# Second attention layer: keys of ten sequences projected around the expert stage and kept on chip

## Chip, cores and metric

One core of one Trainium2 chip. The metric is the device time of one execution in microseconds. Three executions of the kernel before took 968.67, 968.87 and 966.95 us, median 968.67 us. The engines are named as the profile names them: PE (TensorE matmul), PEld (its weight load), DVE (VectorE), ACT (ScalarE), POOL (GpSimd), SP (SyncE, here the main issuer of transfers).

## What is computed

The input is 32 sequences of 128 tokens of width 128 (`x`) and a context of the same shape. Two layers follow each other, each a cross attention and a feed-forward part, each with a layer norm ahead of it and a residual sum behind it. Layer 0: 16 heads of 8 columns, then top-2 of 8 experts (128 to 512 to 128). Layer 1, the one that the change is about:

```python
kv = context @ Wkv
k, v = jnp.split(kv, 2, axis=-1)
q = x @ Wq                                  # 16 heads of 64 columns: 1024 wide
dots = jnp.einsum('bhnd,bhmd->bhnm', q, k) * SCALE
dots = dots - (1.0 - mask.astype(jnp.float32))[:, None, :, None] * MASK_NEG
attn = jax.nn.softmax(dots, axis=-1)
out = jnp.einsum('bhnm,bhmd->bhnd', attn, v)
return out.transpose(0, 2, 1, 3).reshape(b, n, h * d) @ Wout + bout
```

and a feed-forward part of width 512. The keys of layer 1 depend on the context and on `Wkv` alone, not on `x`.

## The kernel before, in words

Everything is fp32. Each engine has its own program, written out by hand; semaphores (`x_ge` waits with counts) tie them together, and each engine works strictly in the order written. There are four stages.

1. **First layer** (`step0`, 32 sequences, a pipeline of some seven steps). Each step also projects the second layer's values of one sequence and stores them in DRAM (`v_dram`). SP loads weights for later stages between blocks of steps (`late_loads`).
2. **First passage.** DVE counts rows for each expert and works out the first tile of each (`tile_start`, L896 to L915), ACT and SP zero the last tile of each expert's rows in DRAM (`zero_last_tile`, L317: a register load and a 128 KB transfer each), PE turns the query mask (L1200), waits for `rt["tiles"]` and loads nine tile counts into registers (L1211), transposes the first tile (`transpose_tile`, L1206) and starts.
3. **Experts** (L1213 to L1227): 35 tiles of 256 rows. PE works as a chain of L1219 (first product), L1206 (transpose of the next tile) and L1226 (second product); ACT applies relu (L685).
4. **Second passage** and **second layer** (`step1`). POOL gathers expert outputs (L563), DVE adds them to `X` (L954) and normalizes; then the steps run.

In `step1`, step n of PE runs, in this order: first half of the scores of sequence n (L1254, S_BANK), a transpose of probabilities (`transpose_unit`, L1066), the output product of n-2 (L1281), the second feed-forward product of n-3 (L1291), another L1066, the transposes of the normalized rows and of the context of n+1 (`transpose_in`, L1056 and L1058), second half of the scores, L1066, the projections `project_y` of n+1 (L1242), the transpose of n-2 for the feed-forward part (L1339), first half of attention times values of n-1 (`values`, L1264), L1066 of n, the second half of L1264, and the first feed-forward product (L1363). `project_y(q, g)` is four matmuls of 128x128 by 128x128; g = 0 and 1 give the keys, g = 2 and 3 the queries. DVE reads each g out of PSUM with `read_y` (L949) into `YT`: g = 0, 1 and then, in the next step, g = 2, 3. g uses banks 4, 5, 6, 4; the two halves of `values` use banks 5 and 6, so they wait until DVE has read g = 1 and g = 2.

ACT's order in a step: copy of transposed probabilities, `fill_rows` (L616, the mask and the move of scores from PSUM to `PR`), `exponentials` (L609) of units 2 and 3 of the sequence before, `read_heads` (L694), `fill_rows` of units 0 and 1, `read_xct` (L597, transposed rows and context), `exponentials` of units 0 and 1 of this one, `fill_rows` of unit 2. DVE takes row maxima (`row_max`, L786), `sums_reciprocal` (L791); POOL scales the probabilities (`scale_pool`, L327). `over_steps` writes the first and last steps out and loops over pairs in between: in `step1` steps -3 to 5 are written out, 6 to 27 are the loop.

## Time and profile before

| | |
|---|---|
| median of three executions | 968.67 us |
| the profiled execution's own time | 973.7 us |
| its span, first to last instruction | 972.1 us |
| PE busy | 903.8 us, 93% of the span |
| DVE, ACT, POOL busy | 675.3, 674.9, 442.4 us |
| mean granted PE clock | 0.977 of full speed |
| first layer, to PE's last piece of it | 0 to 344.3 us |
| first passage (PE without work) | 344.6 to 355.7 us |
| experts | 355.7 to 491.7 us |
| second passage (PE without work) | 491.7 to 502.8 us |
| second layer | 502.8 to 972.1 us |

A row of a timeline gives the start in us, the busy time in us, engine, line of the kernel, operation, output and input tiles with shapes and how many instructions were merged; in brackets stands how long the engine sat idle before it and what released it. An fp32 matmul of 128x128 by 128x128 stands as two records (L1242: 16 matmuls for each of 32 sequences, 1024 records), a transpose as one. Ends of matmuls are modelled: the distance of starts tells more than the duration.

### The profile page before, as it was taken

Reading aid. Unit: us, or ns where it says so; the run is one execution under the profiler, and the core shown is the slowest. Engines: PE = TensorE matmul, PEld = TensorE weight load, DVE = VectorE, ACT = ScalarE, POOL = GpSimd, SP = SyncE. Lnnn points to the kernel's source line nnn. Section 1 sums busy time; section 2 is a strip of 40 time slices with the busy share of each in tenths; the row PEclk is TensorE's granted clock in tenths of the full one; section 3 lists DMA queues with packets and bytes.
Section 4 is the critical chain, followed back from the end, with each engine's and each line's share of the span. In section 5 each row is a group of like instructions: output and inputs, shape, how many; then the busy total and the mean of one; then the engine's idle time right before and its main releaser. Section 6 shows DMA issues by size and latency. Waiting matters only on the chain. (4 is left out here: it accounts for less than half of the span.)

```text
span 972.1 us, 30288 instructions
## 1 busy us (share of the span) xinstructions
PE 903.8 (93%) x8399; PEld 786.3 (81%) x8399; DVE 675.3 (69%) x2169; ACT 674.9 (69%) x2666; POOL 442.4 (46%) x732
## 2 busy tenths in 40 slices
PE   3899999999999849999948999999999999999996
PEld 2577777777777639999947899999999999999986
DVE  5689989899987742222237777777777777777763
ACT  1799989989998703332308877877787787778782
POOL 4033444444343421111145666666666656666542
PEclk9999999999999959999979999999999999999998
DMA  4766667666766222222221121212111211211110
GB/s 136 213 214 209 218 195 233 208 217 208 238 204 208 71 77 72 70 71 70 65 70 58 48 62 59 63 43 65 54 53 54 62 57 43 65 57 62 36 51 9
DMA packets 115276, 103.74 MB, mean 107 GB/s; under 512 B 11921, under 2 KB 102579, under 8 KB 115222
## 3 DMA queue, kind: packets, MB, share of 16 engines
q1 hardware_dynamic: 106754, 88.81, 29.4%
q0 software_dynamic: 5776, 12.99, 4.4%
q10 hardware_dynamic: 2692, 1.31, 0.5%
q8 instruction: 24, 0.39, 0.2%
q14 instruction: 30, 0.25, 0.1%
HBM read 56.53 MB, written 46.53 MB: 106 GB/s over the span
## 5 line engine op out<-in xcount | busy, mean ns | idle before, releaser
L609 ACT ACTIVATE PR<-PR,nmx 128x128 f32<-128x128 f32 x512 | 197.7, 391 | 2.6 <-DVE nmx L786 2.6
L327 POOL TENSOR_TENSOR PR<-PR,rden 128x512 f32<-128x512 f32 x128 | 133.9, 1046 | 129.0 <-DVE rden L791 129.0
L609 ACT ACTIVATE PR<-bank,nmx 128x128 f32<-128x128 f32 x512 | 182.5, 385 | 7.4 <-issue 5.6
L1066 PE MATMUL bank<-ident,PR 128*128 128x128 f32 x1024 | 161.0, 281 | 2.5 <-DVE w L797 1.2
L1066 PEld LDWEIGHTS bank<-ident,PR 128*128 128x128 f32 x1024 | 114.5, 141 | 57.7 <-issue 42.2
L949 DVE COPY YT<-bank 128x512 f32<-128x512 f32 x128 | 84.3, 678 | 56.5 <-PE bank L1242 56.2
L1242 PE MATMUL bank<-XCT,wqk 128*128 128x128 f32 x1024 | 121.4, 277 | 0.5 <-ACT XCT L597 0.5
L1242 PEld LDWEIGHTS bank<-XCT,wqk 128*128 128x128 f32 x1024 | 118.5, 194 | 1.0 <-ACT XCT L597 0.9
L609 ACT ACTIVATION_READ_ACCUMULATOR PR<-bank,nmx 128x1 f32 x512 | 114.5, 224 | 0.0
L685 ACT ACTIVATE H<-bank 128x512 f32<-128x512 f32 x70 | 41.8, 597 | 102.7 <-PE bank L1219 102.7
L786 DVE TENSOR_REDUCE nmx<-bank 128x4 f32<-128x512 f32 x128 | 86.6, 677 | 18.4 <-PE bank L1084 17.8
L609 ACT ACTIVATION_READ_ACCUMULATOR PR<-PR,nmx 128x1 f32 x512 | 98.1, 192 | 0.0
L786 DVE TENSOR_REDUCE nmx<-PR 128x4 f32<-128x512 f32 x128 | 86.4, 676 | 11.0 <-ACT PR L616 11.0
L616 ACT ACTIVATE PR<-bank,fill_q 128x512 f32<-128x512 f32 x128 | 83.9, 679 | 11.1 <-PE bank L1254 7.6
L563 POOL DMA_INDIRECT QF<-expert_outputs,gidx x64 | 65.4, 1022 | 36.5 <-POOL gidx L560 24.4
L597 ACT ACTIVATE XCT<-bank 128x256 f32<-128x256 f32 x64 | 24.6, 385 | 81.8 <-PE bank L1058 81.3
L290 POOL TENSOR_TENSOR rstd<-veps,expo 128x1 f32<-128x1 f32 x128 | 73.2, 572 | 14.6 <-POOL veps L287 8.0
L287 POOL TENSOR_SCALAR veps<-mv 128x1 f32<-128x1 f32 x128 | 29.4, 229 | 104.0 <-DVE mv L303 95.0
L1254 PE MATMUL bank<-YT 64*128 64x128 f32 x1024 | 74.4, 285 | 2.4 <-DVE YT L949 1.2
L1084 PE MATMUL bank<-KBD,QS 128*128 128x512 f32 x128 | 76.2, 595 | 0.0
L549 POOL DMA_DIRECT2D expert_outputs<-PR x35 | 19.0, 543 | 124.6 <-DVE PR L940 124.6
L539 POOL DMA_INDIRECT expert_inputs<-wide,scat_idx x64 | 66.0, 1031 | 16.7 <-issue 10.0
(177 smaller groups left out, 2068.8 us busy)
## 6 DMA issues: line engine op xcount, KB each, us to landing
second_layer_values<-wide SPq DMA_DIRECT2D x32, 512.0 KB, 3.2
wide<-second_layer_values SPq DMA_DIRECT2D x32, 512.0 KB, 3.2
expert_outputs<-HF SPq DMA_DIRECT2D x32, 256.0 KB
expert_outputs<-HF SPq DMA_DIRECT2D x64, 128.0 KB, 1.9
KBD<-expert_outputs SPq DMA_DIRECT2D x128, 64.0 KB
QS<-expert_outputs SPq DMA_DIRECT2D x32, 256.0 KB
PR<-expert_inputs SPq DMA_DIRECT2D x36, 128.0 KB, 2.0
expert_outputs<-PR POOLq DMA_DIRECT2D x35, 128.0 KB, 2.0
```

The lines of the kernel that those rows point to most:

```text
L290: nc.gpsimd.tensor_tensor(rstd[:, p, :], veps[:, p, :], expo[:], ALU.pow).then_inc(s["rstd"], 1)
L327: nc.gpsimd.tensor_tensor(unit, unit, rden[:, p, G * g:G * g + G].unsqueeze(2).broadcast_to([P, G, P]), ALU.mult).then_inc(s["nm"], 1)
L539: nc.gpsimd.indirect_dma_start(xs, bass.IndirectOffsetOnAxis(scat_idx[:, p, k:k + 1], 0), XK[:, p, :], None).then_inc(rt[f"sc{p}"], 16)
L563: nc.gpsimd.indirect_dma_start(GY[:, q, i, :], None, ys, bass.IndirectOffsetOnAxis(gidx[:, q, i:i + 1], 0)).then_inc(mix[f"g{q}"], 16)
L609: last = nc.scalar.activation(PR[:, g, j * P:(j + 1) * P], scored, ACT.Exp, bias=nmx[:, p, h:h + 1], accum_out=den[:, p, h:h + 1])
L616: nc.scalar.activation(PR[:, g, :], S_BANK[g % 2][:], ACT.Identity, bias=fill_q[:, bass.ds(m, 1)]).then_inc(c["sh"], 1)
L786: nc.vector.tensor_reduce(nmx[:, p, G * g:G * g + G], scored.rearrange("p (j k) -> p j k", j=G), AXX, ALU.max, negate=True).then_inc(s["mx ...
L949: nc.vector.tensor_copy(YT[:, p, G * g:G * g + G, :].rearrange("p h s -> p (h s)"), Y_BANK[g][:]).then_inc(c["yc"], 1)
L1066: last = nc.tensor.transpose(T_BANK[g % 2][:, j * P:(j + 1) * P], PR[:, g, j * P:(j + 1) * P], ident[:])
L1084: mm(S_BANK[g % 2][:], QS[:, p, g, :], KBD[:, p, g, :, :].rearrange("p j s -> p (j s)"), start=False, stop=True, skip_group_check=True).th ...
L1242: last = mm(Y_BANK[g][:, j * P:(j + 1) * P], wqk1[:, 1 - g // 2, chunk * P:(chunk + 1) * P], XCT[:, p, 1 - g // 2, :], start=True, stop=True)
L1254: last = mm(S_BANK[r][:, j * P:(j + 1) * P], QT1[half, p, chunk, :], KT1[half, p, chunk, :], start=True, stop=True)
```

## The change

For sequences 0 to 9 (`early`) the keys of layer 1 are no longer projected in their step but ahead of the second layer, by a new function `keys_ahead`, and stay on chip: those of 0 to 4 in the first passage (`KEYS`, in the place of two first-layer tiles), those of 5 to 9 in the second (in the expert weights' tiles `w2` and `w1`). Each group transposes five contexts, ACT copies them to `CT`, 40 matmuls project the keys, and ACT moves each half of a sequence's keys out of PSUM (`read_keys`). Two transfers of 320 KB bring the contexts, into the tiles of the key masks that are no longer read. In their steps these ten sequences transpose no context, project g = 2 and 3 only, and DVE reads only these; everything else keeps its order. ACT does the keys of sequences 1 to 4 between the zeroing transfers. Ten steps of `step1` instead of six (steps -3 to 9) are written out, the loop starts at 10. Some semaphores are merged, with no other effect. Shown with what is left out marked by "...":

```diff
+KEYS_A = 5
+KEYS_AHEAD = 10
...
+        with ExitStack() as first_layer:
+            KBD = first_layer.enter_context(nc.sbuf_tensor("KBD", [P, 2, NU, G, P], FP32R))
+            QS = first_layer.enter_context(nc.sbuf_tensor("QS", [P, 2, NU, P], FP32R))
+        KEYS = sb("KEYS", [P, KEYS_A, PAIRS, P])
...
+        CTX_A, CTX_B = (t[:].bitcast(FP32).rearrange("p (k d) -> p k d", d=P) for t in (mk3, mk_bc))
+        CT = H[:].rearrange("p a c s -> p (a c) s")
+
+        def early(m):
+
+            return isinstance(m, int) and m < KEYS_AHEAD
+
+        def key_slot(m):
+
+            if m < KEYS_A:
+                return KEYS[:, m, :, :]
+            if m < 9:
+                return w2[:, 2 * (m - 5):2 * (m - 5) + 2, :, :].rearrange("p e c d -> p (e c) d")
+            return w1[:, 4:6, :].rearrange("p e (c d) -> p (e c) d", d=P)
...
+                    sp.wait_ge(set_copy, 3)
+                    sp.dma_start(CTX_A[:, 0:KEYS_A, :], ctx_in[0:KEYS_A].rearrange("b s d -> s b d")).then_inc(ld_kv, 16)
...
+            sp.wait_ge(a["kc"], NB)
+            sp.dma_start(CTX_B[:, 0:KEYS_AHEAD - KEYS_A, :],
+                         ctx_in[KEYS_A:KEYS_AHEAD].rearrange("b s d -> s b d")).then_inc(ld_gate, 16)
             sp.wait_ge(rows_zeroed, 3)
             sp.wait_ge(rt["counts"], 1)
...
-                if exists(n + 2):
+                if exists(n + 2) and not early(n + 2):
...
+            act.wait_ge(wo_strips, 2)
+            nc.scalar.activation(fill_q[:], bank[0][:, 0:NB], ACT.Copy).then_inc(parts_ready, 1)
+            def read_keys(m, half):
+
+                act.wait_ge(kg["k"], 2 * m + half + 1)
+                out = (bank[6], bank[5])[half] if m < KEYS_A else bank[half]
+                nc.scalar.activation(key_slot(m)[:, 4 * half:4 * half + 4, :].rearrange("p c s -> p (c s)"), out[:],
+                                     ACT.Copy).then_inc(kg["kc"], 1)
+
+            def read_contexts(group, fifth):
+
+                act.wait_ge(set_pe, group + 3)
+                nc.scalar.activation(CT[:, 0:4, :].rearrange("p c s -> p (c s)"), bank[3][:], ACT.Copy)
+                nc.scalar.activation(CT[:, 4, :], fifth[:, 0:P], ACT.Copy).then_inc(set_copy, 1)
+
+            read_contexts(0, bank[4])
+            read_keys(0, 0)
+            read_keys(0, 1)
+            act.wait_ge(rt["counts"], 2)
             nc.scalar.activation(egap[:], gap[:], ACT.Exp).then_inc(rt["egap"], 1)
-
-
             act.wait_ge(rows_zeroed, 3)
             act.wait_ge(rt["counts"], 1)
             for e in range(1, NE):
                 zero_last_tile(act, e)
+                if e < KEYS_A:
+                    read_keys(e, 0)
+                    read_keys(e, 1)
...
+            read_contexts(1, bank[6])
+            for m in range(KEYS_A, KEYS_AHEAD):
+                for half in range(2):
+                    read_keys(m, half)
...
-                    read_xct(c, n + 1, q, True, c["y"], NU * (n))
+                    read_xct(c, n + 1, q, not early(n + 1), c["y"], NU * (n))
...
-                if exists(n + 1):
+                if exists(n + 1) and not early(n + 1):
                     read_y(n + 1, q, 0)
...
+            def keys_ahead(group, first, last, contexts, fifth, out):
+
+                pe.wait_ge(ld_kv if group == 0 else ld_gate, 32)
+                for i in range(last - first):
+                    turned = nc.tensor.transpose((bank[3][:, i * P:(i + 1) * P] if i < 4 else fifth[:, 0:P]), contexts[:, i, :], ident[:])
+                turned.then_inc(set_pe, 1)
+                pe.wait_ge(set_copy, group + 4)
+                for m in range(first, last):
+                    for half in range(2):
+                        if m > first:
+                            pe.wait_ge(kg["kc"], 2 * m + half - 1)
+                        for j in range(G):
+                            chunk = G * half + j
+                            projected = mm(out[half][:, j * P:(j + 1) * P], wqk1[:, 1, chunk * P:(chunk + 1) * P],
+                                           CT[:, m - first, :], start=True, stop=True)
+                        projected.then_inc(kg["k"], 1)
+
+            pe.wait_ge(ld_w1, 12 * 16)
+            pe.wait_ge(a["x"], NB)
+            pe.wait_ge(a["pjv"], 2 * NB)
+            keys_ahead(0, 0, KEYS_A, CTX_A, bank[4], (bank[6], bank[5]))
...
             transpose_tile(0)
+            pe.wait_ge(kg["kc"], 2 * KEYS_A)
...
+            keys_ahead(1, KEYS_A, KEYS_AHEAD, CTX_B, bank[6], (bank[0], bank[1]))
...
+                    keys = key_slot(m) if early(m) else KT1[:, p, :, :]
+                    if isinstance(m, int) and m == 0:
+                        pe.wait_ge(kg["kc"], 2 * KEYS_AHEAD)
...
-                    transpose_in(c, n + 1, q, True)
+                    transpose_in(c, n + 1, q, not early(n + 1))
...
+                if exists(n + 1) and not early(n + 1):
...
+                    project_y(n + 1, q, 0)
...
+                    project_y(n + 1, q, 1)
                 if exists(n + 1):
...
+                    project_y(n + 1, q, 2)
...
+                    project_y(n + 1, q, 3)
...
-            over_steps(pe, step1, -3, NB + 2, 3, 6)
+            over_steps(pe, step1, -3, NB + 2, 3, KEYS_AHEAD)
```

## Rows read from the trace of the kernel before

**Rows 1.** The page, busy time of the engines, and PE in 40 slices.

```profile
PE 903.8 (93%) x8399; PEld 786.3 (81%) x8399; DVE 675.3 (69%) x2169; ACT 674.9 (69%) x2666; POOL 442.4 (46%) x732
...
PE   3899999999999849999948999999999999999996
```

**Rows 2.** Steps 0 to 4 and 7 of the second layer: window, length, busy time, clock.

```profile
510.24:518.72 8.48, 6.90 (x70) 6.21 (x70) 6.01 (x15) 7.05 (x28) 3.09 (x6) 1.00 0.24 77
518.72:530.30 11.58, 10.42 (x115) 9.17 (x115) 9.86 (x24) 10.70 (x42) 8.05 (x12) 1.00 0.07 18
530.30:544.20 13.90, 13.44 (x141) 12.05 (x139) 10.97 (x25) 11.92 (x45) 8.98 (x13) 1.00 0.18 55
...
558.30:572.94 14.64, 14.17 (x148) 12.97 (x147) 10.65 (x29) 11.14 (x43) 8.19 (x12) 1.00 0.17 55
...
601.14:615.24 14.10, 14.10 (x148) 12.89 (x147) 10.62 (x31) 10.98 (x43) 8.80 (x13) 1.00 0.19 58
```

**Rows 3.** Timeline of PE in step 7 of the second layer.

```profile
605.84 0.27 PE L1056 MATMUL bank<-ident,XN 128*128 128x128 f32 x1
605.95 0.27 PE L1058 MATMUL bank<-ident,CX 128*128 128x128 f32 x1
...
607.74 3.74 PE L1242 MATMUL bank<-XCT,wqk 128*128 128x128 f32 x32
...
611.52 1.09 PE L1264 MATMUL bank<-w,wide 128*64 128x128 f32 x16
...
613.13 1.09 PE L1264 MATMUL bank<-w,wide 128*64 128x128 f32 x16
```

**Rows 4.** Timelines of ACT and DVE in step 7.

```profile
606.26 0.39 ACT L597 ACTIVATE XCT<-bank 128x256 f32<-128x256 f32 x1 [2.04 <-PE bank L1058]
...
609.62 0.67 ACT L616 ACTIVATE PR<-bank,fill_q 128x512 f32<-128x512 f32 x1
...
611.04 1.25 DVE L949 COPY YT<-bank 128x512 f32<-128x512 f32 x2
```

**Rows 5.** First passage: timelines of PE, then of ACT.

```profile
344.32 0.31 PE L1200 MATMUL bank<-ident,mq_f 32*128 32x32 f32 x1
355.73 0.68 PE L1206 MATMUL bank<-ident,PR 128*128 128x128 f32 x2 [11.10 <-issue]
356.93 3.79 PE L1219 MATMUL bank<-PR,w 128*128 128x128 f32 x16 [0.51 <-DVE PR L932]
...
346.57 7.52 ACTq L320 DMA_DIRECT2D expert_inputs<-zero  x7
```

**Rows 6.** Register loads of PE's nine tile counts and of ACT's zeroing; columns: duration ns, first and last start.

```profile
L1211 PEldq TENSOR_LOAD <-tile_start x9: 299/317/502, 349.3 to 355.1; - x9
...
L319 ACTq TENSOR_LOAD <-fill_row x7: 279/300/485, 345.7 to 352.8; - x7
```

**Rows 7.** Second passage and head of the second layer: timeline of PE.

```profile
489.73 1.95 PE L1226 MATMUL bank<-w,H 128*128 128x128 f32 x16
502.84 0.45 PE L1056 MATMUL bank<-ident,XN 128*128 128x128 f32 x1 [11.16 <-DVE XN L295]
...
503.98 5.48 PE L1242 MATMUL bank<-XCT,wqk 128*128 128x128 f32 x32 [0.47 <-ACT XCT L597]
510.24 1.16 PE L1254 MATMUL bank<-YT 64*128 64x128 f32 x16 [0.78 <-DVE YT L949]
```

**Rows 8.** Head of the second layer: timelines of POOL and DVE.

```profile
506.43 0.57 POOL L290 TENSOR_TENSOR rstd<-veps,expo 128x1 f32<-128x1 f32 x1
...
510.10 0.34 DVE L295 TENSOR_SCALAR XN<-X,mv,rstd 128x128 f32<-128x128 f32 x1
...
512.21 1.28 DVE L786 TENSOR_REDUCE nmx<-PR 128x4 f32<-128x512 f32 x2 [0.35 <-ACT PR L616]
```

**Rows 9.** Windows with the granted clock (third column from the right), both passages.

```profile
360.00:361.00 1.00, 1.00 (x8) 1.00 (x7) 0.00 (x0) 0.25 (x1) 0.00 (x0) 0.66 0.00 0
...
492.00:496.00 4.00, 0.00 (x0) 0.00 (x0) 0.01 (x1) 0.00 (x0) 0.82 (x3) 0.72 0.09 33
```

More of the change, by code:

```diff
@@ L668, in _ @@
             nc.scalar.activation(wqk1[:, 0, :], wqk1[:, 0, :], ACT.Copy, scale=float(DH1) ** -0.5).then_inc(wq_scaled, 1)
-            act.wait_ge(c_turned, 1)
-            nc.scalar.activation(fill_q[:], bank[0][:, 0:NB], ACT.Copy).then_inc(c_stored, 1)
-            act.wait_ge(rt["gap"], 1)
+            act.wait_ge(wo_strips, 2)
[13 more added lines that the diff above has]
+            act.wait_ge(rt["counts"], 2)
             nc.scalar.activation(egap[:], gap[:], ACT.Exp).then_inc(rt["egap"], 1)
@@ L897, in _ @@
             nc.vector.tensor_copy(fill_row[:], next_row[:]).then_inc(rt["counts"], 1)
-            nc.vector.tensor_tensor(gap[:], topv[:, 1, :], topv[:, 0, :], ALU.subtract).then_inc(rt["gap"], 1)
+            nc.vector.tensor_tensor(gap[:], topv[:, 1, :], topv[:, 0, :], ALU.subtract).then_inc(rt["counts"], 1)
             link(nc.vector.tensor_tensor(place[:], next_row[:], region[:], ALU.subtract))
@@ L949, in read_y @@
                     nc.vector.tensor_copy(YT[:, p, G * g:G * g + G, :].rearrange("p h s -> p (h s)"),
-                                          Y_BANK[g][:]).then_inc(c["yc"], 1)
+                                          Y_BANK[g][:]).then_inc(c["yc"], 3 if g == 2 and early(m) else 1)
                 def add_experts(m, p, i, done):
@@ L1243, in project_y @@
                                   XCT[:, p, 1 - g // 2, :], start=True, stop=True)
-                    last.then_inc(c["y"], 1)
+                    last.then_inc(c["y"], 3 if g == 2 and early(m) else 1)
                 def scores(m, p, pair):
+                    keys = key_slot(m) if early(m) else KT1[:, p, :, :]
+                    if isinstance(m, int) and m == 0:
+                        pe.wait_ge(kg["kc"], 2 * KEYS_AHEAD)
                     wait(pe, c["yc"], NU * m + NU)
@@ L1253, in scores @@
                             half = slice(DH1 * r, DH1 * r + DH1)
-                            last = mm(S_BANK[r][:, j * P:(j + 1) * P], QT1[half, p, chunk, :], KT1[half, p, chunk, :],
+                            last = mm(S_BANK[r][:, j * P:(j + 1) * P], QT1[half, p, chunk, :], keys[half, chunk, :],
                                       start=True, stop=True)
@@ L1287, in step1 @@
                         wait(pe, c["yc"], upto(n, 4, 3))
-                        wait(pe, c["yc"], upto(n, 4, 0))
+                        if not early(n):
+                            wait(pe, c["yc"], upto(n, 4, 0))
                         wait(pe, d["x"], upto(n - 4))
@@ L1307, in step1 @@
                     transpose_unit(c, n - 1, 3)
-                if exists(n + 1):
+                if exists(n + 1) and not early(n + 1):
                     pe.wait_ge(c["xct"], n + 2)
@@ L1313, in step1 @@
                         wait(pe, c["yc"], upto(n, 4, 3))
-                        wait(pe, c["yc"], upto(n, 4, 0))
-                    project_y(q, 0)
+                        if not early(n):
+                            wait(pe, c["yc"], upto(n, 4, 0))
+                    project_y(n + 1, q, 0)
                     pe.wait_ge(c["xct"], n + 2)
@@ L1318, in step1 @@
                     if isinstance(n, int):
-                        wait(pe, c["yc"], upto(n, 4, 1))
-                    project_y(q, 1)
+                        if not early(n):
+                            wait(pe, c["yc"], upto(n, 4, 1))
+                    project_y(n + 1, q, 1)
+                if exists(n + 1):
                     pe.wait_ge(c["xct"], n + 2)
@@ L1324, in step1 @@
                         wait(pe, c["yc"], upto(n, 4, 2))
-                    project_y(q, 2)
+                    project_y(n + 1, q, 2)
                     pe.wait_ge(c["xct"], n + 2)
-                    wait(pe, c["yc"], upto(n + 1, 4, 0))
+                    if not early(n + 1):
+                        wait(pe, c["yc"], upto(n + 1, 4, 0))
                     if isinstance(n, int):
@@ L1343, in step1 @@
                     pe.wait_ge(c[f"v{q}"], loads(n - 1, q))
-                    wait(pe, c["yc"], upto(n + 1, 4, 1))
+                    if not early(n + 1):
+                        wait(pe, c["yc"], upto(n + 1, 4, 1))
                     if isinstance(n, int):
@@ L1358, in step1 @@
                     if isinstance(n, int):
-                        wait(pe, c["yc"], upto(n + 1, 4, 0))
+                        if not early(n + 1):
+                            wait(pe, c["yc"], upto(n + 1, 4, 0))
                         wait(pe, d["x"], upto(n - 3))
```

39 lines of the change are left out of this document (18 added, 21 removed).

## The prediction

> **What bounds the kernel now.** I read first the page's busy times and slices: PE is busy 93% of the span and falls off in two places only, the passages before and after the experts [rows 1]. Then the windows over single steps of the second layer: from step 3 on PE is busy for all of a step's 14.10 us, while ACT has 10.98, DVE 10.62 and POOL 8.80 us of work [rows 2]. So a step costs what PE issues in it. Steps 0 to 2 differ: 8.48, 11.58 and 13.90 us, PE busy for 6.90, 10.42 and 13.44; in step 1 it is ACT (10.70 of 11.58) that hardly rests [rows 2]. Third, the timelines of the passages: PE does nothing for 11.1 us in each [rows 5, 7]. The first gap is not all free time. Its releaser reads "issue", and the rows of PE's sequencer say why: the nine tile counts are loaded one after another, from 349.3 to 355.1 us, 5.8 us for eight intervals or 0.72 us for each, 6.5 in all, and the first tile is transposed 0.2 us behind the last [rows 5, 6]. The second gap waits for POOL and DVE, up to the first normalized rows at 502.84 [rows 7].
>
> **A step of an early sequence.** Removed from PE: two of four projections, 16 of 32 records. 32 of them take 3.58 us by their starts (3.74 with the modelled end), 0.112 us each, so 1.79 us; and the context's transpose, 0.11 us (605.84 to 605.95) [rows 3]. Together 1.90 us. From DVE go two reads of 0.6 us, from SP a transfer, from ACT half of a small copy; none bounds a full step. Does the whole 1.90 arrive? The second half of L1264 writes the bank from which DVE must have read the first query half. DVE reads that behind a row maximum which needs ACT's `fill_rows`; ACT starts that at 609.62 behind eight exponentials, which start behind the copy at 606.26, which hangs on PE's transpose at 605.84 [rows 3, 4]. That chain keeps its length, but for 0.1 us of a shorter copy: the pair of reads starts at 611.04, the first is done at about 611.67, in the new step at 611.55. PE would be at this L1264 at 613.13 - 1.90 = 611.23 [rows 3]. It waits 0.3 us and a semaphore's passage, say 0.4. So a full early step becomes 12.6 us, a gain of 1.5; ACT with 10.9 of 12.6 still fits. Bounds: 1.9 without that wait, and 0.4 if the others of the queue (transposes behind POOL's scaling, L1254 behind the reads) come short too.
>
> **The sum over the second layer.** The projections of sequence 0 stand in step -1, those of 1 to 9 in steps 0 to 8. *Head:* the first queries are projected warm, 16 x 0.112 = 1.8 us instead of 5.48 [rows 7], so the first scores could start some 4.2 us earlier. But the row maxima behind them stand in DVE's order behind the normalization of sequence 1, which POOL's root allows at 506.43 + 0.57 = 507.0; it happened at 510.10, and the maxima at 512.21 [rows 8]. 2.11 us separate these two, 0.35 of it idle, so the maxima come at about 507.05 + 1.8 = 508.85, 3.4 us earlier. From there ACT works without rest, and step 1 starts 3.4 us earlier. *Step 1* is ACT's: 11.58 goes to 10.3, near its own work; 1.2. *Step 2:* PE's 13.44 less 1.90 is 11.54, and 0.2 of waits: 2.2. *Steps 3 to 8:* six times 1.5, and the 0.5 us that step 4 has over the others (14.64), which comes from a late read that more slack lets vanish: 9.5 [rows 2]. Sum 16.3 us gained. Bounds: 19 with no wait in full steps, 12 with 0.8 a step.
>
> **First passage.** All of `keys_ahead(0)` stands in PE's order ahead of the nine register loads, and these no longer run beside DVE's and POOL's work. From 344.63 [rows 5]: five transposes, at the lower level of the clock (1.2 of 2.4 GHz), for PE was nearly idle before. The first tile, behind its gap, shows what that costs: its first 16 records took 3.58 us (356.93 to the successor's start at 360.51), 0.22 each, and the clock rose in the window 360 to 361 (0.66), 3.5 us into dense products [rows 5, 9]. So 1.1 us; then ACT's two copies, 0.9 us with passages: 346.6. Of 80 records 16 run slow (3.5 us, to 350.1) and 64 at 0.112 (7.2 us): 357.3. ACT reads the keys between zeroings, one in 7.1/6 = 1.18 us, most of it register load, which I let its sequencer run ahead of the copies [rows 5, 6]; for a sequence that is 1.2 beside two copies of some 0.5, against PE's 1.8. I add 0.5: 357.8. Then 6.5 us of loads, 364.3, and the first tile's transposes at 364.4 instead of 355.73: 8.7 us lost. ACT's last three zeroings end at about 361.5, under cover of the loads. The clock will have dropped again, as it began to after the last expert product (0.72 in 492 to 496) [rows 9], so the first tile is slow as before: no change. Bounds: 4.5, if the loads begin under PE's products, and 11 if each zeroing stands in series with its copies (2.2 us a sequence).
>
> The profile shows the loads only with PE idle [rows 6], so I have them begin when the products end. The Trainium skill, in "TensorE: Matmul & The Clock Gate" ("Architectural detail: the array is 16x 32x32"), says that TensorE's queue is 64 deep, so that its sequencer may run on while products are queued. By that the loads would overlap the last half's eight records, and the passage would cost 0.9 us less; no row here shows it.
>
> **Second passage.** PE ends the experts at 491.6. Five transposes 0.6, ACT's copies and passages 0.9: 493.1. 80 records at 0.112 are 9.0 us: 502.1, against 502.75, when the first rows are ready [rows 7]. It fits, with 0.65 us to spare, if the clock stays up over a rest of 1 us; with it up, the head above runs fast. ACT's ten copies of 0.6 us hide beside PE's 0.9 each, the last done at 502.8, before `read_xct` needs ACT. Cost nothing; if one of these is longer by 1 us, up to 0.5. The transfers: 320 KB in the first layer and 320 KB at its end, where SP is idle; two issues, no waiter: nothing, bound 1 us.
>
> **Sum.** -16.3 + 8.7 = -7.6 us. The profiled execution took 973.7 us itself (972.1 of span), 5.0 over the median; it would be 966.1, and the median 968.67 - 7.6 = **961.1 us**.
>
> **Rivals.**
> *A: the loads or the slow clock cost less than I think.* If PE's sequencer passes the products, or the clock is up from the start, the first passage costs 4.5 us. For it: ACT's loads for the zeroings stand in its sequencer's rows, not in its engine's [rows 6]. Against: PE's waits for `kc` hold its sequencer to the last half. With the full 1.9 a step in half of the steps: -4.5 - 14 = -13.5 and so 956.5 or less. 0.2.
> *B: the clock stays low.* If waits for ACT keep it at 1.2 GHz over both groups, the first ends at 345 + 19 + 6.5 = 370.5, 14.8 us late, and in the second 80 records take 17.9, 8.3 us past the rows. -16.3 + 14.8 + 8.3 = +6.8: 975.5. Against: in both PE is dense for its first 3.5 us, and comes into the second at full clock. 0.03. Only the first of them low: -16.3 + 14.8 = -1.5, 967.2; 0.05.
> *C, the slow side: the freed time in the steps turns into the wait at L1264.* The place is the second half of `values`, behind the chain transpose, copy, eight exponentials, `fill_rows`, maximum, read. Its price: if a full step gives 0.2 and steps 1 and 2 give 0.5 together, the layer gives 3.4 + 0.5 + 1.2 = 5.1, and 8.7 - 5.1 = +3.6: 972.3. It decides against the change from where steps 1 to 8 together gain under 5.3 us, 0.66 a step. For it: ACT's slack falls from 3.1 to 1.7 us a step. Against: the chain, timed row by row, leaves only 0.4. 0.1.
> *D: the gain and the price cancel*, 4 us less in steps and 3 more in the passage: about 968. 0.1.
>
> **How the numbers follow.** Forecast 0.52, A 0.2, C 0.1, D 0.1, B 0.03 and its milder form 0.05. The range for 8 in 10: the forecast with its bounds (12 to 19 gained, 7 to 11 lost: 956.7 to 967.7), and most of A: 955.5 to 967.7. 0.2% is 1.9 us, about what a measurement can tell from no change. Faster by over that (below 966.7): forecast and A, and a little of D, 0.74; within it: the rest of D and B's milder form, 0.13; slower (over 970.6): C and B, 0.13.
>
> **What would show it.** In the changed profile: L1211's loads start at 357 to 358 and the first L1206 comes at 364 to 365; the second keys' products end at 502 to 503 on a scale moved by this, and L1056 follows 11 us behind the last L1226; the first maximum is 9 us behind the first L1056 before and 6 after; steps 3 to 8 last 12.6 us with a wait for YT before the second L1264; from step 9 14.10 again. I am wrong if the first tile comes within 3 us of 355.7, if early steps last over 13.4, or if the second passage grows.

## The result: 0.5% slower, and the profile after

The changed kernel takes 973.85 us (median of 7 executions, 971.04 to 974.91) against 968.67 us (966.95 to 969.53): ratio 1.0052, 95% interval 1.0038 to 1.0067, that is 3.7 to 6.5 us more. The forecast was 961.1 us, 7.6 less. The profiled execution took 973.05 us itself, span 971.3 us. It seems shorter than the one shown of before (973.7), but that one was 5 us over its own median, in its first layer: that layer ended at 344.3 us, and in the trace of **e7** below, which shares it, at 340.3. So the two traces are compared piece by piece.

| piece, by the starts of PE's instructions | before, us | after, us | difference | forecast |
|---|---|---|---|---|
| the query mask's turn to the first tile's transpose | 11.41 | 19.74 | +8.3 | +8.7 |
| experts | 134.00 | 133.76 | -0.2 | 0 |
| last second product to the first normalized rows | 13.11 | 14.98 | +1.9 | 0 |
| head and step 0 of the second layer | 15.88 | 12.80 | -3.1 | -3.4 |
| step 1 | 11.58 | 10.88 | -0.7 | -1.2 |
| step 2 | 13.90 | 13.62 | -0.3 | -2.2 |
| steps 3 to 8 | 85.14 | 81.39 | -3.8 | -9.5 |
| from step 9 | 342.7 | 342.7 | 0.0 | 0 |

They sum to +2.1 us. In the first layer a single step is longer, 11.3 us instead of 9.4: together +4.0 us, inside the measured interval. The page after, busy times and PE in 40 slices:

```profile
PE 908.8 (94%) x8399; PEld 790.6 (81%) x8399; DVE 667.3 (69%) x2149; ACT 686.5 (71%) x2690; POOL 441.6 (45%) x732
...
PE   3899999999999769999988889999999999999997
```

PE is busier than before [rows 1], for the same 8399 instructions; work was moved, none left out. The lines of the kernel have moved too. L1256 and L1265 are the transposes and the products of `keys_ahead`, L1284 the register loads (L1211 before), L1279, L1293 and L1300 the experts' (L1206, L1219, L1226), and in the second layer L1107, L1318, L1333, L1343 and L1423 are what L1056, L1242, L1254, L1264 and L1339 were. In the experiments all of them shift by a few lines more. The first passage on PE's timeline, and then the register loads (duration in ns, first and last start):

```profile
341.43 0.31 PE L1251 MATMUL bank<-ident,mq_f 32*128 32x32 f32 x1
341.67 1.33 PE L1256 MATMUL bank<-ident,mk 128*128 128x128 f32 x5
343.85 11.84 PE L1265 MATMUL bank<-H,wqk 128*128 128x128 f32 x80 [0.85 <-ACT H L709]
361.17 0.69 PE L1279 MATMUL bank<-ident,PR 128*128 128x128 f32 x2 [5.48 <-issue]
```

```profile
L1284 PEldq TENSOR_LOAD <-tile_start x9: 293/306/539, 354.7 to 360.5; - x9
```

As forecast, the keys fill the gap of [rows 5] and the nine loads of [rows 6] stand behind them, 5.8 us from the first to the last as before, now with DVE and POOL at rest and ACT done at 359.2. They begin at 354.7 while the 80 records run to 355.7: PE's sequencer runs 1.0 us ahead of its products. The Trainium skill gives TensorE a queue 64 deep ("TensorE: Matmul & The Clock Gate", "Architectural detail: the array is 16x 32x32"), which would have made the passage 0.9 us cheaper than my sum. The overlap agrees with that; how deep the queue is, no run here shows.

Second passage and head: PE, then DVE and SP.

```profile
496.71 0.71 PE L1256 MATMUL bank<-ident,mk_bc 128*128 128x128 f32 x5
498.28 9.44 PE L1265 MATMUL bank<-H,wqk 128*128 128x128 f32 x80 [0.85 <-ACT H L709]
509.91 0.30 PE L1107 MATMUL bank<-ident,XN 128*128 128x128 f32 x1 [2.20 <-DVE XN L302]
510.58 2.05 PE L1318 MATMUL bank<-XCT,wqk 128*128 128x128 f32 x16 [0.37 <-ACT XCT L624]
513.51 1.16 PE L1333 MATMUL bank<-KEYS,YT 64*128 64x128 f32 x16 [0.88 <-DVE YT L1000]
```

```profile
498.55 0.49 DVE L991 COPY PR<-bank 128x128 f32<-128x128 f32 x2 [2.92 <-DMA expert_outputs<-PR]
```

```profile
493.40 0.81 SPq L505 DMA_DIRECT2D wide<-second_layer_values  x2
```

The keys cost nothing here: PE is done 2.2 us before the rows come. But the rows come 1.9 us later than in [rows 7], because DVE waits 2.9 us for a store of expert outputs before it can empty the last tile. At that time two loads of values, 512 KB each, are under way. Before, the first of them was issued at 503.9, 14.2 us behind the last second product; now both are issued ahead of it. The landing times, after and then before (last column, median us):

```profile
wide<-second_layer_values SPq DMA_DIRECT2D x2, 512.0 KB, 4.0
expert_outputs<-PR POOLq DMA_DIRECT2D x2, 128.0 KB, 3.2
```

```profile
expert_outputs<-PR POOLq DMA_DIRECT2D x2, 128.0 KB, 2.0
CX<-in_ctx_dram SPq DMA_DIRECT2D x2, 64.0 KB, 1.9
```

Windows over steps 0, 1, 2, 4, 7 and 10 of the second layer, after (window, length, busy PE, PEld, DVE, ACT, POOL, clock, DMA), and PE in step 7:

```profile
513.51:522.71 9.20, 7.99 (x54) 7.15 (x54) 4.87 (x13) 7.41 (x29) 6.05 (x9) 0.63 0.06 18
522.71:533.59 10.88, 8.59 (x99) 7.29 (x98) 8.23 (x19) 10.16 (x40) 7.39 (x10) 1.00 0.04 12
533.59:547.21 13.62, 11.70 (x125) 10.21 (x123) 10.30 (x26) 11.81 (x45) 9.45 (x14) 1.00 0.16 51
560.49:575.36 14.87, 12.42 (x132) 11.07 (x131) 10.18 (x28) 11.03 (x43) 8.79 (x14) 1.00 0.16 52
601.98:615.29 13.31, 12.42 (x131) 11.07 (x130) 10.20 (x28) 10.94 (x43) 8.80 (x14) 1.00 0.20 61
642.70:656.80 14.10, 14.10 (x149) 12.89 (x149) 10.63 (x31) 10.98 (x43) 8.80 (x13) 1.00 0.19 58
```

```profile
608.47 1.95 PE L1318 MATMUL bank<-XCT,wqk 128*128 128x128 f32 x16
611.31 0.33 PE L1423 MATMUL bank<-ident,XND 128*128 128x128 f32 x1 [0.89 <-DVE XND L317]
611.57 1.09 PE L1343 MATMUL bank<-w,wide 128*64 128x128 f32 x16
```

Against [rows 2] step 7 lost 0.79 us of length where PE lost 1.68 of busy time. PE waits 0.89 us, and it waits at L1423, ahead of the first L1343, not at the second as forecast. L1423 transposes `XND`, the normalized rows of sequence n-2 that go into its feed-forward part. What the wait is for is to be read from POOL, DVE and ACT in the same step:

```profile
606.45 1.08 POOL L590 DMA_INDIRECT QF<-expert_outputs,gidx  x1 [0.79 <-POOL gidx L587]
607.84 0.96 POOL L590 DMA_INDIRECT QF<-expert_outputs,gidx  x1 [0.30 <-issue]
...
609.57 0.57 POOL L297 TENSOR_TENSOR rstd<-veps,expo 128x1 f32<-128x1 f32 x1
610.14 1.03 POOL L334 TENSOR_TENSOR PR<-PR,rden 128x512 f32<-128x512 f32 x1
```

```profile
610.18 1.07 DVE L317 TENSOR_SCALAR XND<-X,mv,rstd 128x128 f32<-128x128 f32 x1 [1.17 <-POOL rstd L297]
```

```profile
610.24 0.67 ACT L643 ACTIVATE PR<-bank,fill_q 128x512 f32<-128x512 f32 x1
610.81 0.58 ACT L650 ACTIVATE w<-bank 128x512 f32<-128x512 f32 x1
```

Two things hold PE up, and they arrive 0.1 us apart. XND needs POOL's norm, and POOL does it behind two gathers; it is written at 611.25. And the first L1343 needs all transposed probabilities of n-1, whose last copy (L650) stands in ACT's order behind eight exponentials and `fill_rows`; it is done at 611.39. Before, PE came to L1264 at 611.52, 5.7 us behind its L1056 (605.84), with both ready; now it could come 3.9 us behind and comes 4.9 behind (611.57, with L1107 at 606.68). The same two rows before, in step 7:

```profile
609.53 0.32 DVE L310 TENSOR_SCALAR XND<-X,mv,rstd 128x128 f32 x1
610.19 0.58 ACT L623 ACTIVATE w<-bank 128x512 f32<-128x512 f32 x1
```

XND took 0.32 us there and takes 1.07 in every one of the changed kernel's steps 2 to 8, where POOL's scaling (L334) begins 0.05 us ahead of it. So 0.75 of the 0.89 us that PE waits for XND is XND's own length, and ACT's copy would hold PE almost as long. The copy is of the fourth unit, which only the second half of L1343 reads; the program lets the first half wait for all four. No run tried a narrower wait.

### The profile page after: what moved, and what is told of

It reads as the page before. It is cut to its first block and busy times, and to the rows that moved or that the text cites. A ratio compares the mean times of both kernels' runs of the same rounds, so it can differ in the third digit from the quotient of the medians.

```text
span 971.3 us, 30078 instructions
## 1 busy us (share of the span) xinstructions
PE 908.8 (94%) x8399; PEld 790.6 (81%) x8399; DVE 667.3 (69%) x2149; ACT 686.5 (71%) x2690; POOL 441.6 (45%) x732
## 5 line engine op out<-in xcount | busy, mean ns | idle before, releaser
L334 POOL TENSOR_TENSOR PR<-PR,rden 128x512 f32<-128x512 f32 x128 | 133.7, 1044 | 122.1 <-DVE rden L842 122.0
L1318 PE MATMUL bank<-XCT,wqk 128*128 128x128 f32 x864 | 103.7, 278 | 0.4 <-ACT XCT L624 0.4
L1318 PEld LDWEIGHTS bank<-XCT,wqk 128*128 128x128 f32 x864 | 100.6, 195 | 0.8 <-ACT XCT L624 0.6
L837 DVE TENSOR_REDUCE nmx<-bank 128x4 f32<-128x512 f32 x128 | 86.6, 677 | 16.9 <-PE bank L1135 16.2
L1000 DVE COPY YT<-bank 128x512 f32<-128x512 f32 x108 | 70.7, 677 | 39.0 <-PE bank L1318 38.9
L837 DVE TENSOR_REDUCE nmx<-PR 128x4 f32<-128x512 f32 x128 | 86.4, 676 | 12.3 <-ACT PR L643 12.2
L624 ACT ACTIVATE XCT<-bank 128x256 f32<-128x256 f32 (+1 forms) x64 | 23.5, 367 | 69.7 <-PE bank L1109 55.2
L1343 PE MATMUL bank<-w,wide 128*64 128x128 f32 x1024 | 69.8, 279 | 1.1 <-issue 1.1
```

The lines of the kernel that those rows point to most:

```text
L334: nc.gpsimd.tensor_tensor(unit, unit, rden[:, p, G * g:G * g + G].unsqueeze(2).broadcast_to([P, G, P]), ALU.mult).then_inc(s["nm"], 1)
L837: nc.vector.tensor_reduce(nmx[:, p, G * g:G * g + G], scored.rearrange("p (j k) -> p j k", j=G), AXX, ALU.max, negate=True).then_inc(s["mx ...
L1000: nc.vector.tensor_copy(YT[:, p, G * g:G * g + G, :].rearrange("p h s -> p (h s)"), Y_BANK[g][:]).then_inc(c["yc"], 3 if g == 2 and early( ...
L1318: last = mm(Y_BANK[g][:, j * P:(j + 1) * P], wqk1[:, 1 - g // 2, chunk * P:(chunk + 1) * P], XCT[:, p, 1 - g // 2, :], start=True, stop=True)
L1343: last = mm(bank[5 + pair][half, j * P:(j + 1) * P], V1[:, p, 2 * (G * pair + j) + r, :], PTC[:, 2 * pair + r, j * P:(j + 1) * P], start=T ...
```

## The experiments

Ratios are to the kernel before on the same chip, with 95% intervals. Chips differ: before took 968.7 us on the first, 986.5 on that of the second set, 969.5, 970.3 and 985.4 on the next; the difference is in the first layer (on that of the second set it ended at 357.4 instead of 344.3 us), the rest is equal to 0.1 us a step.

### Where the time is: before once more, values held back, counts late

**e0_before_again** is the kernel before, unedited.

> The kernel before, unchanged, profiled and timed once more. The medians say that the change costs 5.2 us, while the two traces, laid over each other by the events of PE, give -2.9 us in the first layer, +8.3 in the first passage, +1.9 in the second, -7.8 in the second layer. Theory: the first trace of before had a first layer 3 to 5 us longer than usual; a new trace of the same kernel then ends its first layer at 339 to 341.5 us instead of 344.3, and the ratio is 1.000 within 0.002. Rival: first layers of before always end at about 344, and the change makes something else slower that the two traces do not show.

Ratio 1.0001 (0.9987 to 1.0015). Passage 11.23, second passage 13.11, steps 14.10: these repeat. The first layer cannot be compared, as the chip was another. What it was meant to test is settled by e7 below, which has the first layer of before on a chip where before takes 969.5 us: it ended at 340.32, not 344.32. The changed kernel's ended at 341.43 in its trace and at 340.8 to 345.9 in those of e5, e8, e9 and e10, so traces of one kernel differ by some 4 us there.

**e1_hold_values**

```diff
                 if exists(n + 2) and not early(n + 2):
                     load_ctx(sp, c, n + 2, p)
+                elif exists(n):
+                    wait(sp, c["tr"], n + 1)
```

> The changed kernel, with SP again holding each of the first loads of values until the transpose that released it before (the context load that carried this wait is gone). Theory: the two loads of 512 KB at 493.4 us stood in the way of the last stores of the expert outputs, which DVE and POOL wait for; held back, the second passage shrinks from 15.0 to 13.1 us and the time falls by 1.9 us against the changed kernel (973.85), to about 972. Rival: the passage grew because ACT or PE is busy with keys; then it stays at 15.0.

Ratio 1.0018 (1.0007 to 1.0030) where the change has 1.0052. The second passage is 13.16 us, and POOL's stores come every 3.79 us up to the last, which in the changed kernel came 5.63 us behind the one before (494.17 to 499.80):

```profile
513.88 0.54 POOL L578 DMA_DIRECT2D expert_outputs<-PR  x1 [3.25 <-DVE PR L993]
517.67 0.54 POOL L578 DMA_DIRECT2D expert_outputs<-PR  x1 [3.25 <-DVE PR L993]
```

The passage's 1.8 us (14.98 to 13.16) are shown to be the two loads. The ratio fell by 3.3 us, more than that; the two intervals leave room for it. The context loads that the change took away had carried the wait that kept the values behind them.

**e3_late_counts**

```diff
-            starts = [pe.value_load(tile_start[0:1, e:e + 1], ...) for e in range(NE + 1)]
+            low = pe.value_load(tile_start[0:1, 0:1], ...)
             transpose_tile(0)
...
             for e in range(NE):
-                with pe.Fori(starts[e], starts[e + 1]) as t:
+                high = pe.value_load(tile_start[0:1, e + 1:e + 2], ...)
+                with pe.Fori(low, high) as t:
...
+                low = high
```

> The changed kernel, with PE loading only the first two tile counts ahead of the experts and each further one ahead of its expert's loop. Theory: the nine loads in series behind the keys are 6.5 us of the first passage's 19.7; with two of them left it is 14.7, and each of the seven moved loads shows for at most 0.7 us between two experts, less what queued products hide: 1 to 5 us less than the changed kernel in all. Rival: the first passage waits for ACT's keys, its zeroing or the transfer of the first tile; then it stays at 18 or more.

Ratio 1.0010 (0.9996 to 1.0025). The first passage is 13.92 us instead of 19.74: the loads were 5.8 us of its growth. The experts take 135.0 us instead of 133.8, but with unedited experts they take 133.6 to 135.0 too, by how long the clock stays at 1.2 GHz in the first tile (5.3 to 6.7 us to the second). What the moved loads give back is read from the tiles behind it: 14 of them last 3.83 to 3.87 us instead of 3.79, 0.9 us in all. That is 4.1 us less than the changed kernel by the ratio, as expected.

### The held steps: four orders of POOL, then ACT and DVE

**e2_pool_order**

```diff
+                if exists(n - 2):
+                    norm_pool(pool, d, n - 2, p)
+                if exists(n) and exists(n - 2):
+                    scale_pool(pool, c, n, p, 0)
                 if exists(n + 3):
                     ...                      # the gathers
...
-                if exists(n - 2):
-                    norm_pool(pool, d, n - 2, p)
-                if exists(n):
+                if exists(n) and not exists(n - 2):
                     scale_pool(pool, c, n, p, 0)
```

> The changed kernel; in each step of the second layer POOL does the norm of n-2 and the first scaling of n ahead of the two gathers, not behind them. Theory: early steps last 13.31 us instead of 12.2 because XND waits for POOL, which stands in two gathers of 3.3 us; with this order the wait of 0.9 us ahead of L1423 vanishes and early full steps last 12.4 to 12.7 us, steps behind them 14.10 as before: 5 to 6 us less than the changed kernel, about 968. Rival: the next wait (ACT's chain to the queries' read, at the second L1343) takes its place at the same length; then steps stay at 13.3.

1027.87 us on a chip where before takes 986.5, ratio 1.042 (1.040 to 1.044). The expectation would be some 986 us there: a miss by 42 us. Early steps last 14.1 to 16.2, late ones 15.1 to 16.2 us. From 600 to 800 us DVE waits for the gathers once, 0.2 us, so they are not what is late. It waits for POOL's second norm, that of a later sequence, for which it doesn't wait there in the changed kernel. The waits of e2 from 700 to 800 us:

```profile
DVE XN L302 <- POOL rstd L297: 14.3, 6, 2.4
```

In this order the scaling stands ahead of the gathers and of that norm, and POOL waits at its scalings for DVE's reciprocals (up to 2.5 us), so all behind it comes late. This is read from the waits; no run tried the norm without the scaling.

**e5_gathers_last** and **e7_before_gathers_last**: the gathers at the end of POOL's step, from step 0 on, in the changed kernel and in that of before.

```diff
-                if exists(n + 3):
+                def gather():
                     ...                      # index copy and both gathers
+                late = not isinstance(n, int) or n >= 0
+                if exists(n + 3) and not late:
                     gather()
...
                     nc.gpsimd.tensor_tensor(xrow, xrow, out_bias[:, 1, :], ALU.add).then_inc(d["bias"], 1)
+                if exists(n + 3) and late:
+                    gather()
```

> The changed kernel; from step 0 on POOL issues its two gathers at the end of a step instead of behind the first scaling. (With the norm and a scaling moved ahead of them, every step of the layer had become longer, 14.2 to 16.2 us.) Theory: XND no longer waits for the gathers, the norm of n-2 is done about 2 us earlier, and the wait ahead of L1423 goes: early full steps last 12.3 to 12.7 us, late steps 14.10; 4 to 6 us less than the changed kernel, ratio to before 1.000 plus or minus 0.001. Rival: XND is late because of the output product and DVE, or the next wait takes its place; then early steps stay at 13.3.

> The kernel before with the same move of POOL's gathers as in e5_gathers_last. Theory: its full steps are PE's, 14.10 us with XND ready 1.5 us ahead of its use, so the order of POOL changes nothing: ratio 1.000 plus or minus 0.001, steps 14.10. Rival: gathers cost steps of the kernel before too, and what e5 gains has nothing to do with the change; then this one gains as much.

Ratios 1.194 (1.192 to 1.197) and 1.191 (1.189 to 1.194): steps of some 20 us in both. The waits of e7 from 600 to 700 us name it:

```profile
DVE X L961 <- DMA QF<-expert_outputs,gidx: 34.0, 5, 7.9
```

```profile
642.39 0.35 DVE L961 SCALAR_TENSOR_TENSOR X<-QF,gate,X 128x128 f32 x1 [6.60 <-DMA QF<-expert_outputs,gidx]
```

DVE adds the gathered rows ahead of much else in its order. It is free for that at 635.8 us, and POOL issues these gathers at 638.25 and 639.63; every step waits up to 7.9 us for them. Both expectations were wrong: the end of POOL's step, taken as early enough, is too late for DVE. No run put the gathers earlier.

**e8_norm_between_gathers** (only in steps with an early next sequence), **e9_copy_early** and **e10_three_orders** (both, and the queries' first half read where the keys' was):

```diff
# e8, POOL
                     for i in range(2):
                         nc.gpsimd.indirect_dma_start(GY[:, q, i, :], ...)
+                        if i == 0 and early(n + 1) and exists(n - 2):
+                            norm_pool(pool, d, n - 2, p)
...
-                if exists(n - 2):
+                if exists(n - 2) and not early(n + 1):
                     norm_pool(pool, d, n - 2, p)
# e9, ACT
-                if exists(n - 2):
+                if exists(n - 2) and not early(n):
                     read_PT(c, n - 2, 3)
...
                     exponentials(c, n, p, 0)
+                if exists(n - 1) and early(n + 1):
+                    read_PT(c, n - 1, 3)
# e10, DVE besides
-                    read_y(n, p, 2)
+                    if not early(n):
+                        read_y(n, p, 2)
...
-                if exists(n + 1) and not early(n + 1):
-                    read_y(n + 1, q, 1)
+                if exists(n + 1):
+                    read_y(n + 1, q, 2 if early(n + 1) else 1)
```

> The changed kernel; in steps whose next sequence is early, POOL does the norm of n-2 between its two gathers (gathers moved to the end of a step came too late for DVE's sum, which waited 8 us for them). Theory of two waits: an early step is held by two things that arrive within 0.1 us of each other, XND (POOL's norm behind both gathers; DVE at 611.25 in the changed trace) and ACT's copy of transposed probabilities (L650, done 611.38), for the first L1343 at 611.57. Freeing XND alone gives nothing: steps 5 to 8 stay within 13.1 to 13.3 us. Rival: XND alone holds the step; then steps are 12.3 to 12.7 us. Step 4's 14.87 stays (a POOL pause of 2.3 us ahead of its gather).

> The changed kernel; in early steps ACT makes the copy of the fourth unit's transposed probabilities between its two groups of exponentials instead of behind fill_rows. Theory of two waits: alone it gives nothing either, since XND is still late: steps 5 to 8 at 13.2 to 13.5 us. Rival: ACT's copy alone holds the step; then steps are 12.8 or less.

> Both moves together, and DVE reads the first query half in the place where it read the first key half. Theory of two waits: now PE finds XND, the copy and the queries' read ready, and an early full step is 12.2 to 12.6 us: 0.7 to 1.1 us a step, 5 to 7 us less than the changed kernel in all, ratio 0.998 to 1.000. Rival: a further chain (ACT's 10.9 us of work a step, or POOL's scaling) holds the step near 13; then the gain is under 2.5 us.

| | step 2 | 3 | 4 | 5 | 6 | 7 | 8 | ratio |
|---|---|---|---|---|---|---|---|---|
| changed | 13.62 | 13.28 | 14.87 | 13.31 | 13.31 | 13.31 | 13.31 | 1.0052 |
| e8 | 12.51 | 13.29 | 13.42 | 13.23 | 13.23 | 13.24 | 13.23 | 1.0018 (1.0003 to 1.0033) |
| e9 | 13.69 | 13.28 | 15.17 | 13.34 | 13.55 | 13.33 | 13.57 | 1.0072 (1.0044 to 1.0100) |
| e10 | 12.44 | 12.32 | 15.93 | 12.20 | 12.95 | 12.34 | 12.80 | 0.9997 (0.9979 to 1.0015) |

Each alone leaves a full step where it was (e9's sixth and eighth are 0.2 us longer), both (with the read) take 0.4 to 1.1 us off steps 3 and 5 to 8; 12.2 to 12.6 was expected, and three of the five are in it. In e10 PE goes through without a stop to the first values:

```profile
610.71 1.95 PE L1324 MATMUL bank<-XCT,wqk 128*128 128x128 f32 x16
612.50 0.27 PE L1429 MATMUL bank<-ident,XND 128*128 128x128 f32 x1
612.70 1.09 PE L1349 MATMUL bank<-w,wide 128*64 128x128 f32 x16
```

In its even steps something third holds PE, a transpose that waits for POOL's scaling. Step 6:

```profile
601.52 0.66 PE L1123 MATMUL bank<-ident,PR 128*128 128x128 f32 x4 [0.64 <-POOL PR L334]
```

Step 4 keeps a pause of POOL (below), and behind PE's waits there the clock is at 1.2 GHz for some 3 us; with the same orders step 4 of e11 stays at full clock and lasts 14.37. Step 4 of e10:

```profile
563.14:579.07 15.93, 14.05 (x131) 12.32 (x130) 12.01 (x31) 12.20 (x47) 10.27 (x15) 0.89 0.19 55
```

The traces show the two waits one by one. In e9 the copy is early, and PE waits for XND as before (step 7). In step 5 of e8 XND is done at 582.52, 1 us before PE asks for it, and PE waits as long for ACT's copy. The steps are 13.33 and 13.23 us:

```profile
614.51 0.33 PE L1426 MATMUL bank<-ident,XND 128*128 128x128 f32 x1 [0.91 <-DVE XND L317]
```

```profile
582.17 0.35 DVE L317 TENSOR_SCALAR XND<-X,mv,rstd 128x128 f32<-128x128 f32 x1
584.06 0.58 ACT L652 ACTIVATE w<-bank 128x512 f32<-128x512 f32 x1
584.74 1.09 PE L1345 MATMUL bank<-w,wide 128*64 128x128 f32 x16 [0.96 <-issue]
```

In steps 3 and 6 to 8 of e8 XND is not free. It starts 1.3 us earlier against the step, but ends only 0.1 earlier. DVE and POOL of step 7:

```profile
608.64 2.25 DVE L317 TENSOR_SCALAR XND<-X,mv,rstd 128x128 f32<-128x128 f32 x1
```

```profile
608.24 1.08 POOL L590 DMA_INDIRECT QF<-expert_outputs,gidx  x1 [0.19 <-issue]
609.34 0.47 POOL L597 TENSOR_TENSOR X<-X,out_bias 128x128 f32<-128x128 f32 x1
609.75 1.05 POOL L334 TENSOR_TENSOR PR<-PR,rden 128x512 f32<-128x512 f32 x1
```

An instruction of 0.3 us lasts 2.25 us and ends with POOL's third in a row; in the changed kernel it lasted 1.07, beside one L334, and in e10 0.34, begun while POOL rested. The Trainium skill, "SBUF — State Buffer" ("Who interferes with whom"), says that DVE in a two-port mode and POOL take one pair of ports for a whole instruction and the other is blocked. The rows agree, and show besides that the blocked one can miss several in a row; in which mode XND runs, they don't show. So freeing XND pays nothing while the copy is late (e8, steps 4 and 5), freeing the copy pays nothing while XND is late (e9), and both pay together (e10). How much of e10 is the DVE read was not tried apart. The 3.3 us by which e8 is faster than the changed kernel come from steps 2 and 4, against its expectation for step 4.

### The parts of the change: first group out, contexts late

**e4_no_first_group**: `KEYS_AHEAD = 5`, `KEYS_A = 0`; no group ahead of the experts, the five sequences behind them.

```diff
-KEYS_A = 5
-KEYS_AHEAD = 10
+KEYS_A = 0
+KEYS_AHEAD = 5
...
-            keys_ahead(0, 0, KEYS_A, CTX_A, bank[4], (bank[6], bank[5]))
...
-                sp.dma_start(CTX_A[:, 0:KEYS_A, :], ...)
```

> The change with its second group alone: sequences 0 to 4 are projected behind the experts, the first group, its 320 KB of contexts and its place ahead of the experts are gone. Theory: the first passage is back at 11.3 us (8.4 less), the first layer loses its 1.9 us step, steps 4 to 8 are 14.10 us again (3 us more), so about 7 us less than the changed kernel and 2 us less than before, ratio 0.996 to 0.999. Rival: the first group pays for itself; then this is no faster than the changed kernel, ratio 1.005.

Ratio 0.9990 (0.9973 to 1.0007): about 6 us less than the whole change, and not to be told from before. The first passage is 11.72 us, steps from 5 on 14.10; step 4 is 15.42, longer than expected. As built, the first group costs more than it gives.

**e6_contexts_late**: the transfer of the first group's contexts moved from `late_loads` to the end of the first layer.

> The changed kernel with the first group's 320 KB of contexts loaded at the end of the first layer, ahead of those of the second group, instead of in its middle. Theory: in the three traces with that load the twelfth step of the first layer lasts 10.8 to 12.9 us where it is 9.4 (or 9.9 on the second chip) without; that step is back at its usual length, and the time falls by 1.5 to 2 us, ratio 1.003 to 1.004 to before. Rival: the long step is a chance of these traces; then the ratio stays at 1.005.

Ratio 1.0030 (1.0013 to 1.0046), 2 us less. SP's context loads mark the steps of the first layer. In the changed kernel the step behind the extra transfer (L402) is long:

```profile
139.78 0.43 SPq L402 DMA_DIRECT2D mk<-in_ctx_dram  x1
...
148.99 0.37 SPq L322 DMA_DIRECT2D CX<-in_ctx_dram  x1
...
160.19 0.37 SPq L322 DMA_DIRECT2D CX<-in_ctx_dram  x1
...
169.46 0.37 SPq L322 DMA_DIRECT2D CX<-in_ctx_dram  x1
```

11.2 and then 9.3 us. Over the eight traces that have it the twelfth step lasts 10.8 to 13.4 us, over those of before 9.4 (9.9 on the slower chip), in e4 9.7; in e6 still 10.3, for no reason that I found, and 9.4 again in e11, which loads late too. A mean of some 2 us for a transfer that I had put at nothing. By the ratio alone e6 isn't clear of the changed kernel, as the two intervals overlap; the steps show it.

### All together

**e11_all** is e10 with e1's, e3's and e6's edits; **e12_all_second_group** the same with e4's; **e13_before_late_counts** the kernel before with e3's edit alone.

> The three orders, with the value loads held back, the first group's contexts loaded late, and the tile counts loaded one expert ahead. By the traces of the single edits: first passage 13.9 us (19.7), experts 0 to 1 longer, second passage 13.1 (15.0), first layer 1 to 2 shorter, early steps 6 shorter: 13 to 15 us less than the changed kernel, 8 to 10 less than before, ratio 0.989 to 0.992. Rival: the single gains do not add, because each uncovers the next wait; then the ratio is over 0.995.

> e11_all without the first group (sequences 0 to 4 projected behind the experts, none ahead of them). By the traces the first passage goes from 13.8 to about 9.8 us (landing of the first tile bounds it), the experts and the second passage stay, and steps 4 to 8 of the layer go back from 12.3 to 14.4 to 14.1: 4.0 us less and some 7.5 more. Theory (the loss lay in what the group made late): 3 to 4 us slower than e11, ratio to before 0.993 to 0.996. Rival (a loss in itself): as fast as e11 or faster, ratio 0.991 or less.

> The kernel before with only the tile counts loaded one expert ahead. The first passage is bound by the landing of the first tile at about 353.9 instead of the loads at 355.7, so it shrinks by 1.5 to 1.8 us, and the seven moved loads give back 0.5 to 1.3 us among the experts: ratio 0.998 to 1.000. So under a tenth of what e11 gains would come without the change. Rival: the moved loads are hidden altogether and the passage gains more; ratio under 0.998.

| | first passage | experts | second passage | steps 3 to 8 | ratio |
|---|---|---|---|---|---|
| e11 | 13.76 | 134.99 | 13.17 | 77.0 | 0.9905 (0.9886 to 0.9923) |
| e12 | 9.69 | 135.78 | 13.16 | 84.9 | 0.9937 (0.9922 to 0.9953) |
| e13 | 9.88 | 135.36 | 13.19 | 85.2 | 0.9995 (0.9984 to 1.0006) |

e11 takes 959.59 us against 970.29 on its chip and beats both kernels, by 9 us by the ratio (the medians lie 10.7 apart). The single gains do add: by the ratios e1, e3, e6 and e10 gave 3.3, 4.1, 2.1 and 5.3 us against the changed kernel, 14.8 together, and e11 gives 14.3. e12 is 3 us behind it on the ratio, on another chip and with intervals that just touch; the pieces agree with it (4.1 us less of passage, 7.9 more of steps). So with the loads out of the way the first group is worth having. e13 shows that the late counts alone are worth nothing that can be told in the kernel before: its passage is 1.3 us shorter than e0's, and the moved loads give 0.9 back.

## Why the prediction was wrong

**First passage: right.** +8.3 for +8.7, with the nine serial loads as its cause; e3 shows them. The closeness is in part luck: the clock stayed low for 4.7 us of the products instead of 3.5, which made them 0.6 us longer than forecast, and the loads began 1.0 us before the products' end, as rival A had it.

**Head and steps 0, 1: near.** -3.8 for -4.2 to the first scores, 3.1 for 3.4 to step 1, 0.7 for 1.2 in it, where ACT works 10.16 of 10.88 us, the limit as said.

**Steps 2 to 8: the step that failed most.** The prediction named one chain and put its wait at the second half of L1264, 0.4 us. PE stopped earlier, ahead of the first half, 0.89 us in full steps. "none bounds a full step" counted busy time of engines; what bound the step was the place of two instructions in the orders of POOL and ACT. XND and the last copy of probabilities were done 4.6 and 4.7 us behind the step's first transpose (L1107), and PE could now come to its values 3.9 us behind it. The prediction names neither. The rows of before, shown above, had both: XND was written at 609.85 and the copy at 610.77, 4.9 us behind L1056, and would have forbidden a first half at 611.52 - 1.90 = 609.62. From the copy alone, L1264 comes at some 610.8 and a full step lasts 13.4 us, an estimate from these rows; 12.6 was forecast and 13.31 measured. That XND took 1.07 us instead of 0.32 was not to be seen in the step that I read. Term: -11.7 forecast for steps 2 to 8, -4.0 measured. Rival C had this side, with the wait in the wrong place: its threshold was a gain of under 5.3 us in steps 1 to 8, and they gained 4.7.

**Second passage: wrong term.** "It fits" held for PE and ACT. What was missed is on SP: a load taken away had carried a wait, and two loads behind it in the queue ran off into the expert stores, the first 15.7 us early against the end of the experts. The prediction said of SP only that a transfer goes and that it is idle there. 0 forecast, 1.9 measured, 1.8 explained by e1. Of the prediction's own signs of being wrong, this growth is the one that came.

**Transfers: wrong term.** "no waiter: nothing, bound 1 us" was wrong of the one in mid first layer; SP's queue also feeds the steps of that layer, and the step behind the transfer is longer in all eight traces that have it. Which wait in the step it lengthens stays open. 0 forecast, some 2 measured.

**The sum.** 7.6 less forecast, 5.2 more measured: 12.8 us apart. 7.7 of it lies in steps 2 to 8, 1.9 in the second passage, about 2 in the first layer, 0.8 in head and step 1; the first passage and the experts go 0.6 the other way. That leaves 1.0, within the interval of the measurement. One sum of the prediction doesn't come out: in rival A, -4.5 - 14 is not -13.5, and 13.5 us less would be 955.2, not 956.5. Only the lower end of the range touches it.

What stays open is a pause of POOL between an index copy and its gather in step 4. It lasts 2.35 us in all sixteen traces, before and after, where it is 0.8 in other steps. What the step pays for it depends on what else waits: 14.64 us before, 14.87 in the changed kernel, 13.42 in e8.

## What to carry to other kernels

When the engine that is always busy gets less work per step, list for each of its later instructions when its inputs are ready, and count from the event that the whole chain hangs on: the gain ends at the earliest of them, and two that lie close must be moved together. When a transfer is taken out of a queue, ask which wait it carried, for what stood behind it will run early. And work put into a gap costs what it pushes out of the gap: here nine register loads that nobody had seen because they ran beside a wait.

## What was not expected of the hardware

The blocked XND above: 0.32 to 0.35, 1.07 or 2.25 us for one instruction, by what POOL runs as it starts.

PE's clock in the head of the second layer varies between executions that issue the same work. The 16 records of the first queries took 2.05 us in the changed kernel (row above), and in e6:

```profile
509.57 3.78 PE L1318 MATMUL bank<-XCT,wqk 128*128 128x128 f32 x16 [0.37 <-ACT XCT L624]
```

In both PE had rested about 2.3 us behind dense keys. In e6 it had fallen to 1.2 GHz by then, and the first scores came 5.5 us behind the first rows instead of 3.6; in the changed kernel it was still up at 514.5 and down by 516.5, and step 0 ran at 0.63. So one cannot count on the keys behind the experts to keep the clock up.
